# Group norm earlier and on GpSimd, a constant folded into the division, VectorE's sums in pieces: one change to a two-layer network kernel

## The reference

```python
x = x + _L0_attn_ref(_layernorm(x, axis=-1), ...)          # softmax attention, 16 heads of 8
x = x + _L1_attn_ref(_layernorm(x, axis=-1), ...)          # attention with random features, 16 heads
# of the second:
q = jnp.einsum('bnd,dhk->bnhk', x, Wq)
qf = ratio * (jnp.exp(data_dash - diag - mx) + EPS_KERN)    # features of q, mx: maximum over features
num = jnp.einsum('bnhm,bhmd->bnhd', qf, kv)
den = jnp.einsum('bnhm,bhm->bnh', qf, jnp.sum(kf, axis=1))
attn = num / den[..., None]
out1 = _layernorm(x + attn_out, ln1_g, ln1_b)
h = jax.nn.elu(out1 @ W1 + b1)
return _layernorm(out1 + h @ W2 + b2, ln2_g, ln2_b)
```

## Time and profile before

| what | value |
|---|---|
| time, median of 3 runs (lowest to highest) | 3748.41 us (3748.16 to 3749.34) |
| the profiled execution: its own time | 3760.07 us |
| the profiled execution: its span | 3758.2 us |
| its mean granted PE clock, share of full | 0.856 |
| busy share: PE, DVE, ACT, POOL | 85%, 72%, 43%, 20% |
| first attention: first and last reduction L690 | 473.7 us, 1314.2 us |
| queries' stage: its first and last DVE instruction | 2606.4 us, 3456.6 us |

### The profile page before, as it was taken

One profiled execution on the slowest core, in us unless ns is written; L12 is line 12 of the kernel. 1 busy time (PEld: TensorE's weight loads), 2 busy tenths in 40 slices (PEclk: granted clock), 3 DMA queues, 4 the chain that ended last, 5 costly groups with the idle time before them and its releaser, 6 DMA issues. The chain is left out here.

```text
span 3758.2 us, 46804 instructions
## 1 busy us (share of the span) xinstructions
PE 3180.1 (85%) x16466; PEld 1955.5 (52%) x16466; DVE 2698.4 (72%) x6533; ACT 1622.8 (43%) x2274; POOL 734.6 (20%) x693
## 2 busy tenths in 40 slices
PE   7999789999999989999776478887988888885774
PEld 5666434343333436666565345554555555553663
DVE  6778588878778817787558677775677777775567
ACT  3443227667666754444333233333333333332333
POOL 2111111111111001111112222322112221112223
PEclk9999859989888969999755599998999999997555
DMA  1000122122212101000000000000000000000000
GB/s 68 1 1 1 35 92 86 56 78 83 76 58 83 47 11 39 1 1 1 1 0 1 1 12 17 23 17 34 18 12 6 12 12 12 12 1 1 1 12 34
DMA packets 33697, 99.04 MB, mean 26 GB/s; under 512 B 4184, under 2 KB 4792, under 8 KB 29240
## 3 DMA queue, kind: packets, MB, share of 16 engines
q1 hardware_dynamic: 31288, 91.85, 6.7%
q10 hardware_dynamic: 2176, 4.19, 0.3%
HBM read 53.56 MB, written 42.47 MB: 26 GB/s over the span
## 5 line engine op out<-in xcount | busy, mean ns | idle before, releaser
L690 DVE TENSOR_REDUCE att_mx<-att_pair 128x2 f32<-128x1024 f32 x512 | 617.9, 1222 | 165.9 <-PE att_pair L936 165.8
L862 ACT ACTIVATE att_pt<-att_pair 128x1024 f32<-128x1024 f32 x512 | 523.5, 1026 | 285.4 <-PE att_pair L946 282.9
L958 PE MATMUL att_o<-att_pt,att_vx 128*32 128x256 f32 x4096 | 369.0, 450 | 9.1 <-ACT att_oT L868 5.1
L936 PE MATMUL att_pair<-att_k,att_q 24*128 24x512 f32 x1024 | 287.9, 567 | 43.2 <-DMA att_k<-att_spread_k 14.3
L946 PE MATMUL att_pair<-att_q,att_k 26*128 26x512 f32 x1024 | 285.7, 560 | 9.8 <-DVE att_mx L690 9.6
L946 PEld LDWEIGHTS att_pair<-att_q,att_k 26*128 26x128 f32 x1024 | 105.0, 204 | 232.6 <-issue 188.8
L449 ACT ACTIVATE ffnA_h<-ffnA_up,b 128x512 f32<-128x512 f32 x144 | 99.1, 688 | 189.4 <-PE ffnA_up L105 184.8
L449 ACT ACTIVATE ffnB_h<-ffnB_up,b 128x512 f32<-128x512 f32 x144 | 99.1, 689 | 188.2 <-PE ffnB_up L105 182.9
L958 PEld LDWEIGHTS att_o<-att_pt,att_vx 128*32 128x32 f32 x4096 | 95.7, 117 | 157.2 <-issue 140.1
L936 PEld LDWEIGHTS att_pair<-att_k,att_q 24*128 24x128 f32 x1024 | 105.9, 206 | 120.0 <-ACT att_pt L862 73.1
L2275 PE MATMUL att1q_acc<-att1q_qf,att1q_mem 128*128 128x512 f32 x256 | 133.7, 604 | 18.9 <-DVE att1q_qf L2041 17.6
(11 more groups left out here) (560 smaller groups left out, 8272.6 us busy)
## 6 DMA issues: line engine op xcount, KB each, us to landing
att_q<-att_spread_q SPq DMA_DIRECT2D x16, 1024.0 KB, 5.0
att_k<-att_spread_k SPq DMA_DIRECT2D x16, 1024.0 KB, 4.8
att_spread_q<-att_qhi SPq DMA_DIRECT2D x32, 256.0 KB, 2.5
att_spread_k<-att_khi SPq DMA_DIRECT2D x32, 256.0 KB, 3.3
context<-att1k_ctx SPq DMA_DIRECT2D x16, 512.0 KB, 2.6
att1q_cin<-context SPq DMA_DIRECT2D x16, 512.0 KB, 3.3
X<-L_attn_x ACTq DMA_DIRECT2D x8, 512.0 KB, 7.7
att_spread_q<-att_qlo SPq DMA_DIRECT2D x16, 256.0 KB, 2.5
```

What stands on the lines that cost most here:

```text
L690: v.tensor_reduce(top[b % 2][:, t, h:h + 2], pair("s", k)[:, :].rearrange("p (h n) -> p h n", h=2), AX, ALU.max).then_inc(mx, 1)
L862: a.activation(pt[k % 8][:, :, :].rearrange("p h n -> p (h n)"), pair("t", k)[:, :], ACT.Exp, scale=scale).then_inc(p_, 1)
L936: last = pe.matmul(pair("s", k)[:, (j - j0) * 512:(j - j0 + 1) * 512], qb[b % 3][r, u, t * P:(t + 1) * P], kb[b % 3][r, u, :], start=True, ...
L958: last = pe.matmul(obank[j * BLOCK:(j + 1) * BLOCK, cols], vxb[b % 3][:, t, 4 * u + j, :], pt[(2 * g + j // 2) % 8][:, j % 2, cols], start ...
```

## The change

Three edits in two stages.

1. Queries. Every group now starts 16 slots earlier (`AHEAD`): slots -16 and -15 hold the statistics on DVE and, on POOL, the root and now also the application of the norm, which DVE did in slot 4. The other slots keep their places. 
2. Queries. The eight additions of EPS_KERNEL per group (L2020) are gone. The constant is added in the multiplication of slot 62 to 76, which becomes a scalar_tensor_tensor, (f + EPS) * reciprocal. The denominators, which PE now computes from features without the constant, get it as a bias: before the first step PE multiplies the mask with `ksum` (16 columns for all groups), ACT scales the result by EPS_KERNEL into `keps`, and the copy of the denominators (slot 53) becomes an Identity with that bias.
3. First attention. The statistics of the norm are taken in pieces: two tiles after n = 20, two after n = 22, the aggregation after n = 29 (before: all after n = 28). The reduction gives the negated maximum, and the split of the maxima takes two instructions on all tiles in place of eight.

```diff
@@ attn0, vector
-        def sums(b):
-            norm_stats(v, st, nb, b, xg(b), 1e-5, var)
+        def stats(b, t0, t1):
+            for t in range(t0, t1):
+                stated.at(v.bn_stats(nb.stats[b % 2][:, t, :], xg(b)[:, t, :]))
+
+        def moments(b):
+            v.wait_ge(stated.sem, TILES * (b + 1))
+            for t in range(TILES):
+                m = st.at(v.bn_aggr(nb.mv[b % 2][:, t, :], nb.stats[b % 2][:, t, :]))
+            v.wait_ge(st.sem, m)
+            v.tensor_scalar(nb.rstd[b % 2][:, :], nb.mv[b % 2][:, :, 1], 1e-5, None, ALU.add).then_inc(var, 1)
...
-            for t in range(TILES):
-                m = st.at(v.tensor_scalar(rows[:, t, :, 0:8:2], tp[:, t, :, :], -1.0, None, ALU.mult))
-            v.wait_ge(st.sem, m)
-            for t in range(TILES):
-                last = v.scalar_tensor_tensor(rows[:, t, :, 1:8:2], tp[:, t, :, :], -1.0, rows[:, t, :, 0:8:2].bitcast(F32), ALU.mult, ALU.subtract)
-            last.then_inc(mt, 1)
+            m = st.at(v.tensor_copy(rows[:, :, :, 0:8:2], tp))
+            v.wait_ge(st.sem, m)
+            v.tensor_tensor(rows[:, :, :, 1:8:2], tp, rows[:, :, :, 0:8:2].bitcast(F32), ALU.subtract).then_inc(mt, 1)
...
+                if n == 20 and m + 2 < groups:
+                    stats(m + 2, 0, 2)
+                if n == 22 and m + 2 < groups:
+                    stats(m + 2, 2, TILES)
...
-                if n == 28 and m + 2 < groups:
-                    sums(m + 2)
+                if n == 29 and m + 2 < groups:
+                    moments(m + 2)
@@ attn1_queries
-QLEAD, QSLOTS = 40, 122
+QLEAD, QSLOTS, AHEAD = 40, 122, 16
...
-    steps = QLEAD * (groups - 1) + QSLOTS
+    steps = QLEAD * (groups - 1) + QSLOTS + AHEAD
+    at = lambda step: ((i, s - AHEAD) for i, s in live(step, 0, groups, QSLOTS + AHEAD, QLEAD))
@@ vector
-                if s == 0:
+                if s == -AHEAD:
+                    if i >= 2:
+                        v.wait_ge(norm0, i - 1)
                     norm_stats(v, st, nb0, i, xg(i), 1e-5, var0)
-                if s == 4:
-                    v.wait_ge(root0, i + 1)
-                    norm_apply(v, nb0, i, xv, xg(i)).then_inc(norm0, 1)
...
-                if 35 <= s < 51 and s % 2 == 1:
-                    n = PAIRS * i + (s - 35) // 2
-                    f = qfb[n % 12][:, :]
-                    v.wait_ge(qf, n + 1)
-                    v.tensor_scalar(f, f, EPS_KERNEL, None, ALU.add).then_inc(qe, 1)
...
-                    v.wait_ge(qe, n + 1)
-                    v.tensor_tensor(f, f, bank_of("div", i, c)[:, :], ALU.mult).then_inc(div, 1)
+                    v.wait_ge(qf, n + 1)
+                    v.wait_ge(den, i + 1)
+                    v.scalar_tensor_tensor(f, f, EPS_KERNEL, bank_of("div", i, c)[:, :], ALU.add, ALU.mult).then_inc(div, 1)
@@ pool
-                if s == 1:
+                if s == 1 - AHEAD:
                     p.wait_ge(var0, i + 1)
                     norm_root(p, nb0, i, K).then_inc(root0, 1)
+                    p.wait_ge(root0, i + 1)
+                    if i >= 3:
+                        p.wait_ge(y1, i - 2)
+                    norm_apply(p, nb0, i, group(xn[i % 3][:, :]), xg(i)).then_inc(norm0, 1)
@@ scalar
+        a.wait_ge(esummed, 1)
+        a.activation(keps[:, 0:groups], acc[:, 0:groups], ACT.Copy, scale=EPS_KERNEL).then_inc(epsed, 1)
...
-                    a.activation(denT[:, :], acc[:, :], ACT.Copy).then_inc(dT, 1)
+                    a.activation(denT[:, :], acc[:, :], ACT.Identity, bias=keps[:, i:i + 1]).then_inc(dT, 1)
@@ tensor
-                pe.wait_ge(qe, PAIRS * i + c + 1)
+                pe.wait_ge(qf, PAIRS * i + c + 1)
...
+        pe.wait_ge(summed, 1)
+        for part in range(2):
+            for j in range(4):
+                c = 4 * part + j
+                last = pe.matmul(acc[j * STRIP:(j + 1) * STRIP, 0:groups], T["mask"][:, c, :], ksum[:, 0:groups, c], start=part == 0, stop=part == 1)
+        last.then_inc(esummed, 1)
```

More of the change, by code:

```diff
@@ L1979, in vector @@
         v.wait_ge(st.sem, m)
[L1980 removed]
+        v.tensor_scalar(ksum[:, 0:groups, :], ksum[:, 0:groups, :], GROUP * EPS_KERNEL, None, ALU.add).then_inc(summed, 1)
         for step in range(steps):
[L1982 removed]
+            for i, s in at(step):
                 tp, d_, xv, ov, rv = tops[i % 2], dgb[i % 2], group(xn[i % 3][:, :]), group(y1b[i % 2][:, :]), group(y2b[:, :])
[L1984 removed]
+                if s == -AHEAD:
+                    if i >= 2:
+                        v.wait_ge(norm0, i - 1)
                     norm_stats(v, st, nb0, i, xg(i), 1e-5, var0)
[L1986 to L1988 removed]
                 if s == 8:
@@ L2092, in pool @@
         for step in range(steps):
-            for i, s in live(step, 0, groups, QSLOTS, QLEAD):
+            for i, s in at(step):
                 ci, ov, rv = cin[i % 2], group(y1b[i % 2][:, :]), group(y2b[:, :])
-                if s == 1:
+                if s == 1 - AHEAD:
                     p.wait_ge(var0, i + 1)
                     norm_root(p, nb0, i, K).then_inc(root0, 1)
+                    p.wait_ge(root0, i + 1)
+                    if i >= 3:
+                        p.wait_ge(y1, i - 2)
+                    norm_apply(p, nb0, i, group(xn[i % 3][:, :]), xg(i)).then_inc(norm0, 1)
                 if s == 9:
                     if i == 0:
-                        p.wait_ge(begun.sem, begun.n)
+                        p.wait_ge(begun, 4)
+                        p.wait_ge(shifted, 1)
+                        p.wait_ge(summed, 1)
                     p.wait_ge(loaded[i % 2], 16 * (i // 2 + 1))
@@ L2125, in scalar @@
     def scalar(a):
-        a.wait_ge(begun.sem, 3)
-        begun_exp = a.activation(shift[:, 0:groups], T["nmax"][:, 0:groups], ACT.Exp, scale=-1.0, bias=nm[:, :])
-        begun_exp.then_inc(begun.sem, 1)
+        a.wait_ge(begun, 4)
+        a.activation(shift[:, 0:groups], T["nmax"][:, 0:groups], ACT.Exp, scale=-1.0, bias=nm[:, :]).then_inc(shifted, 1)
+        a.wait_ge(esummed, 1)
+        a.activation(keps[:, 0:groups], acc[:, 0:groups], ACT.Copy, scale=EPS_KERNEL).then_inc(epsed, 1)
         for step in range(steps):
-            for i, s in live(step, 0, groups, QSLOTS, QLEAD):
+            for i, s in at(step):
                 if s == 7:
@@ L2250, in tensor @@
                         pe.wait_ge(yt, i)
+                    else:
+                        pe.wait_ge(epsed, 1)
                     denominators(i, 0)
```

32 lines of the change are left out of this document (17 added, 15 removed).

## The result

The changed kernel takes 3598.18 us, the median of 4 runs (3591.45 to 3618.38); the kernel before, in 4 runs of the same comparison, 3748.28 (3743.23 to 3749.34). The ratio is 0.9611, with a 95% interval of 0.9571 to 0.9651: 150 us less. The profiled execution of the changed kernel took 3600.62 us, 159.5 less than that of before. Its stages account for this. The first attention takes 897.8 us where it took 960.2 (62.4 less), the queries 752.5 where they took 850.8 (98.3 less), and the others together are within 2 us of before.

The account below looks back on a forecast made before the run. PE, busy 85% of the span at mean clock 0.856, loses time where it waits and its clock is low. Gains of 94.5 (queries) and 48.6 (first attention), 143.1 us, take the median from 3748.4 to 3606; range 3590 to 3655.

Parts of the forecast that it names:

- The queries: Queries' stage: 6.6 us at each of 14 places, 92.4, plus 1.3, 1.6 and -0.8 elsewhere: 94.5 less.
- Each step of the chain: Queries: from PE's turn of the result through y1, variance, root and af1 to the turn of y; 6.6 us sooner.
- the new wait: Queries: PE waits about 1 us for att1q_y in 14 groups, in place of the old wait for xn.
- rival (b): Queries: the clock still falls at the new wait, 18 us lost: 3624; chance 8%.
- 1.12 a group: Queries: y1 starts 1.12 us sooner on DVE because the addition L2020 in its way is gone.
- The first attention: First attention: 12 PE waits for mx and the low clock behind them go, plus 1.4 for the maxima: 48.6 less.
- Rival (a): First attention: the clock stays low without the wait, so only the waits go, gain 105.6 in all: 3643; chance 18%.
- The maxima: First attention, maxima on two instructions: 1.4 us gained in the first block, bounds 0 and 1.9; elsewhere hidden behind PE.
- Rival (c): Queries: POOL's extra 3.13 us per group lands on the path, 44 us in all: 3650; chance 7%.
- wherever it falls: Queries, within Rival (c): by the shared-port rule POOL's application would hold DVE up at any place, to the full 3.13 us.
- (d): Queries: PE less busy between denominators and af1, clock low far into the next group, slower: 3812; chance 3%.
- (e): Queries: xn early, but another equal wait at the same place; only the first attention gains: 3700; chance 2%.

Follow-up runs that it names:

- q_only: The kernel before with the first two edits alone (queries): 3649.46 us, ratio 0.9755.
- q_ahead_dve: The kernel before with both queries edits, but the norm, 16 slots ahead, applied on VectorE instead of GpSimd: 3650.28 us, ratio 0.9756.
- q_ahead_only: The kernel before with the norm 16 slots ahead on GpSimd (first edit), the eight additions per group kept: 3701.59 us, ratio 0.9885.
- q_ahead_fill: Against q_ahead_only, the last of eight chunks of shift and maxima computed three times over per group, just before PE's wait: 3690.05 us, ratio 0.9836.
- att_whole: The kernel before with the third edit's new maxima, but the statistics whole after n = 28: 3751.72 us, ratio 1.001.
- Both fillers: Step 30's two score matmuls repeated in the first attention, in the kernel before (3720.36 us) and in the changed kernel (3582.95, again 3588.32).
- the filler: The changed kernel with step 30's two score matmuls done twice in each first-attention block: 3582.95 us, ratio 0.9582; again 3588.32, ratio 0.9578.
- fill_before: The kernel before with step 30's two score matmuls done three times over in each first-attention block that has a norm: 3720.36 us, ratio 0.9913.
- affine_dve: The changed kernel with gain and bias of the norm of y moved from GpSimd to VectorE: 3613.82 us, ratio 0.9628.

## Why the prediction was right

**The time.** Predicted 3606, range 3590 to 3655, measured 3598.2.

**The queries** (94.5; measured 98.3 in the stage, and 102 and 93 in the medians of q_only and q_ahead_dve). Each step of the chain came as written: y1 at turn + 0.64 (predicted 0.65), variance to root 0.08 (0.08), `af1` at +7.80 (7.82), turn of `y` at +7.86 (7.9), the new wait 1.01 (about 1). Between the two turns the gain is 14.45 - 7.86 = 6.59, as predicted (6.6). A whole group gained 7.0. The other 0.4, at the last multiplication, the sum did not have; over 14 groups it is 5 to 6 us, more than the 3.8 by which the sum was short, because the ends of the stage gave about 0.6 and not the 2.1 that I had for them.

One reading in this chain was right in size and wrong in its reason. `y1` followed the turn 1.17 late not because of an addition's length; that is 0.43. The addition waits for ACT until 2929.00, and the sum into X stands behind it and ahead of `y1` (2929.94):

```profile
2929.00 0.43 DVE L2020 TENSOR_SCALAR att1q_qf<-att1q_qf 128x512 f32<-128x512 f32 x1 [1.74 <-ACT att1q_qf L2160]
2929.34 0.69 DVE L2082 TENSOR_TENSOR X<-X,att1q_y 128x512 f32<-128x512 f32 x1
```

With the additions gone, that sum runs earlier and is out of the way, too (L2089, at 2875.93 in the group that turns at 2878.38).

**The step that was weak** is the reason that I gave against rival (b), that a wait of 3.04 with no next group left the clock up. It did there; but q_ahead_only shows a wait of 2.65 in the steady groups that brings it down in each, at 1.5 us by q_ahead_fill. The forecast held since the new wait is only 1.0, which nothing in the argument had shown to be short enough; in this it was luck. This is also why the edits don't add up: alone they give 48 and 13 us of stage, together 98. I had treated the constant's folding as 1.12 a group (16 in all). On top of the norm ahead it is worth 50: 1.7 of chain, 1.5 of clock and 0.35 at the last multiplication in each group. Alone it is worth 13, since `xn` still ends the gap and the clock stays at half for longer.

**The first attention** (48.6; the runs of the third edit alone 46). The mechanism was half right. The waits went, and it took the pieces for that (att_whole). But the low clock did not simply follow the wait. In the seven profiles with the old statistics the blocks took 835.7 to 852.5, mean 845.0; in the three with the pieces and no filler 791.5 to 804.8, mean 799.9: 45 less. The sum came out since two errors met. Quiet blocks are 49.85 apart, about 0.5 less than the 50.4 that I had; and some still fall, for 3.4 to 5.0 each: 5 of 14 intervals in the changed kernel's profile, 3 in that of the third edit alone. Rival (a) in pure form, all falls stay, is refuted; in part it is true. Both fillers speak for what PE does at the block's end as the cause, which DVE's lateness only deepens; whether it is the light work there or the stand of 0.26 for ACT in each block, no run separates, since the filler takes both away. The Trainium skill (TensorE: Matmul & The Clock Gate, section What's actually happening) calls throttled the default and activity what releases it; fill_before agrees, where more work at the same lateness made the kernel 31 us faster. The 37 in the profiled pair's blocks, with 25 in the tail, is one draw of each, and the sum had no term for the tail.

**The maxima** (1.4 in the first block, else hidden): att_whole, 1.001 (0.9982 to 1.0038), shows nothing, as bounded.

**Rival (c)**, GpSimd's work on the path, did not come: with it on VectorE the stage takes 753.8 against 752.2. POOL's application lies beside reductions and multiplications, and these are as long beside it as elsewhere (the reduction L2014 1.21 in all 64 cases, the multiplication L2048 0.67 to 0.69). So "wherever it falls", in the prediction, was too wide. The stretching exists, as affine_dve's 2.34 for 1.12 shows, where it hits the chain; before, it also hit the additions (0.43 alone, up to 1.27 beside GpSimd). **(d)** and **(e)** did not come.

**Left open**: why the clock of the tail differs from run to run, what exactly at the block's end brings the clock down, and whether the filler's 10 to 15 us are real.

## What to carry to other kernels

Where PE waits for one engine in each period, write down the whole chain to the next thing that PE needs, with what stands ahead of each link in its engine's queue: here taking foreign instructions out of two queues (a root on POOL, additions and another group's norm on DVE) gave 7 us of 51. An instruction that itself waits costs those behind it more than its length. Price a wait of PE together with the clock behind it, and test that with a few repeated matmuls in the gap or just ahead of it: if adding work makes it faster, the gap cost more than its length. Two edits on one chain are not worth the sum of their single values; measure them together and one by one.
